# A norm moved out of the queries and into the exponential's scale, in a fused Mamba and local-attention kernel

## The reference, cut to what matters

```python
q = l2norm(q) * qs          # t / max(norm(t), 1e-12), per token and head
k = l2norm(k) * ksc
q, k = rotary_xpos(q, k)    # linear in q and in k
sim = einsum(q * 8.0, k)    # per head, 128 queries x 256 keys
sim = where(mask, -max, sim)
attn = softmax(sim)
out = einsum(attn, v)
```

## Time and profile before

| | us |
|---|---|
| median of 3 runs | 2109.19 (2108.12 to 2111.52) |
| the profiled execution, by the clock of the runs | 2109.78 |
| its span, first to last instruction | 2108.0 |
| PE busy | 1957.7 (93%) |
| DVE busy | 1866.4 (89%) |
| ACT busy | 1675.6 (79%) |
| POOL busy | 1094.0 (52%) |

### The profile page before, as it was taken

How to read it: one execution, slowest core, us unless ns; L and a number is a source line. 1 busy time by engine, 2 the same in 40 slices (tenths; PEclk the granted TensorE clock), 3 DMA queues, 4 the chain that set the end, 5 groups by cost and what they waited for, 6 DMA issues and landing times. The chain is left out here.

```text
span 2108.0 us, 40069 instructions
## 1 busy us (share of the span) xinstructions
PE 1957.7 (93%) x12096; PEld 1341.7 (64%) x12096; DVE 1866.4 (89%) x2502; ACT 1675.6 (79%) x4124; POOL 1094.0 (52%) x1214
## 2 busy tenths in 40 slices
PE   6788999999999999999999999999999999998897
PEld 2465666666666666666675666666666666665666
DVE  3988999999999999999989999999999999898881
ACT  4866888878878888888879788897887888887672
POOL 3544554655545655555555555465554565545440
PEclk9989999999999999999999999999999999999999
DMA  4788899789896898888987898978889789788772
GB/s 159 175 216 194 185 245 226 179 194 239 193 250 169 189 250 191 220 200 216 225 213 192 199 222 219 229 190 201 233 197 251 171 194 247 163 212 214 205 150 53
DMA packets 131844, 425.26 MB, mean 202 GB/s; under 512 B 13584, under 2 KB 34832, under 8 KB 113072
## 3 DMA queue, kind: packets, MB, share of 16 engines
q0 software_dynamic: 64512, 184.58, 47.8%
q1 hardware_dynamic: 67120, 238.12, 33.8%
HBM read 241.76 MB, written 155.71 MB: 189 GB/s over the span
## 5 line engine op out<-in xcount | busy, mean ns | idle before, releaser
L761 DVE TENSOR_TENSOR_SCAN hb<-dA,state,hb 128x512 f32<-128x512 f32 x512 | 668.5, 1306 | 36.3 <-ACT dA L934 20.8
L1170 POOL DMA_DIRECT2D ysum<-dA x256 | 222.6, 878 | 375.4 <-DVE dA L768 343.8
L934 ACT ACTIVATE dA<-dt_sb,par 128x512 f32<-128x512 f32 x512 | 349.2, 729 | 12.4 <-DMA ysum<-dA 11.1
L1154 POOL COPY state<-hb 128x2 f32<-128x2 f32 x256 | 207.4, 810 | 255.4 <-DVE hb L761 255.4
L754 DVE TENSOR_TENSOR hb<-u_sb,bc 128x1024 f32<-128x1024 f32 x256 | 316.0, 1234 | 25.6 <-DMA bc<-bc_rows 11.5
L768 DVE TENSOR_TENSOR dA<-hb,bc 128x1024 f32<-128x1024 f32 x256 | 312.2, 1220 | 0.0
L1485 PE MATMUL ring<-hT,w 128*128 128x256 f32 x1280 | 294.9, 388 | 5.2 <-ACT hT L1082 4.1
L1036 ACT ACTIVATE rot<-rot,rnorm 128x64 f32<-128x64 f32 x1024 | 256.5, 341 | 45.1 <-POOL rnorm L1239 43.3
L1485 PEld LDWEIGHTS ring<-hT,w 128*128 128x128 f32 x1280 | 243.9, 193 | 56.3 <-ACT hT L1082 19.0
L1239 POOL TENSOR_TENSOR rnorm<-rnorm,powers 128x8 f32<-128x8 f32 x128 | 265.5, 2075 | 23.5 <-POOL rnorm L1236 22.2
L1061 ACT ACTIVATE probs<-ring,nmax 128x256 f32<-128x256 f32 x512 | 234.8, 481 | 34.5 <-DVE nmax L840 34.1
(11 more groups left out here) (122 smaller groups left out, 3536.9 us busy)
## 6 DMA issues: line engine op xcount, KB each, us to landing
bc<-bc_rows SPq DMA_DIRECT2D x128, 1024.0 KB, 6.0
ysum<-dA POOLq DMA_DIRECT2D x256, 512.0 KB, 7.3
rot<-sq POOLq DMA_DIRECT2D x128, 256.0 KB, 6.3
wqkv<-in_wqkv SPq DMA_DIRECT2D x48, 512.0 KB, 7.3
w<-in_w SPq DMA_DIRECT2D x16, 1408.0 KB, 11.2
w<-in_w SPq DMA_DIRECT2D x16, 896.0 KB, 10.8
tab<-in_tab SPq DMA_DIRECT2D x64, 128.0 KB, 8.4
wo<-in_wo SPq DMA_DIRECT2D x16, 512.0 KB, 9.9
```

The source lines that it names most:

```text
L761: dve.tensor_tensor_scan(hb[:, k % H_RING, :], dA[:, k % DA_RING, :], hb[:, k % H_RING, :], state[:, k:k + 1], ALU.mult, ALU.add).then_inc ...
L934: act.activation(dA[:, k % DA_RING, :], dt_sb[:, j, :], ACT.Exp, scale=par[:, C_ALOG + n:C_ALOG + n + 1]).then_inc(dA_ready.sem, 1)
```

## The change: what it does, and the diff

The scores are linear in q, so 1/norm of a query can be applied to a whole row of scores. The change leaves the queries unscaled: ACT's `turn` runs for k only, and PE transposes q as soon as the two products of the rotation are added. The exponential takes 1/norm of its query and head as its scale, exp(scale * score - scale * maximum). For its bias the negated row maximum must be scaled too; that is a new small DVE product on 128x4 numbers, `mr` (function `scale_max`), two for a window, into a new buffer `shifts`. It waits for the two row maxima, for q's 1/norm, and for the exponentials of the window before, and ACT's `e` waits for it. q's 1/norm is now needed until the last exponential, so it has two buffers that alternate, and POOL's `turn(q,a)` waits for the exponentials of window a-2 where it waited for ACT's norm of window a-1. The tables of all five engines are new.

```diff
-    rnorm = sb("rnorm", [P, 2 * HEADS])
+    rnorm = sb("rnorm", [P, 3 * HEADS])
+    shifts = sb("shifts", [P, HEADS])
...
+            def scale_max(a, c):
+                dve.wait_ge(*nmax_ready.at(it, a * PAIRS + 2 * c + 2))
+                dve.wait_ge(*rnorm_ready.at(it, 2 * a + 1))
+                dve.wait_ge(*probs_ready.at(it, (a - 1) * HEADS + 4 * c + 4))
+                part = slice(4 * c, 4 * c + 4)
+                slot = a % 2 * HEADS + 4 * c
+                dve.tensor_tensor(shifts[:, part].rearrange("p (o h) -> p o h", o=2),
+                                  nmax[:, part].rearrange("p (o h) -> p o h", o=2),
+                                  rnorm[:, slot:slot + 4].rearrange("p (h o) -> p o h", o=2), ALU.mult).then_inc(shifts_ready.sem, 1)
...
-            def norm_heads(name, a):
+            def norm_heads(a):
-                i = "qk".index(name)
+                i = 1
...
                     act.activation(rot[:, i, h * DH:(h + 1) * DH], rot[:, i, h * DH:(h + 1) * DH], ACT.Copy,
-                                   scale=rnorm[:, i * HEADS + h:i * HEADS + h + 1]).then_inc(normed.sem, 1)
+                                   scale=rnorm[:, 2 * HEADS + h:2 * HEADS + h + 1]).then_inc(normed.sem, 1)
...
             def exps(a, g):
                 c, hh = divmod(g, 2)
-                act.wait_ge(*nmax_ready.at(it, a * PAIRS + 2 * c + 2))
+                act.wait_ge(*shifts_ready.at(it, 2 * a + c + 1))
...
-                                   bias=nmax[:, 2 * p + hh:2 * p + hh + 1], accum_out=rowsum[:, head:head + 1])\
+                                   bias=shifts[:, 2 * p + hh:2 * p + hh + 1],
+                                   scale=rnorm[:, a % 2 * HEADS + head:a % 2 * HEADS + head + 1], accum_out=rowsum[:, head:head + 1])\
...
             def scale_heads(name, a):
...
-                pool.wait_ge(*normed.at(it, HEADS * (n - 1)))
+                if i:
+                    pool.wait_ge(*normed.at(it, HEADS * a))
+                else:
+                    pool.wait_ge(*probs_ready.at(it, HEADS * (a - 1)))
...
             def heads(a):
                 for i, name in ((1, "kT"), (0, "qT")):
-                    pe.wait_ge(*normed.at(it, HEADS * (2 * a + i + 1)))
+                    if i:
+                        pe.wait_ge(*normed.at(it, HEADS * (a + 1)))
+                    else:
+                        pe.wait_ge(*rot_added[0].at(it, D16 * (a + 1)))
```

The tables move nearly every row. Of DVE's steady table, one line before and after:

```diff
-stats(3) +scan +scan +m(0,0) +m(0,1) +turn(q,1) +m(0,2) +m(0,3) +scan gate(1) +scan h(3,0) h(3,1) +scan
+o(7) +scan stats(3) +scan +scan +m(0,0) +m(0,1) +mr(0,0) +turn(q,1) +turn(k,1) +m(0,2) +m(0,3) +mr(0,1)
```

More of the change, by code:

```diff
@@ L94 @@
[L94 to L98, removed]
@@ L102 @@
++scan +h(2,0) +h(2,1) +rinv(6) +h(2,2) +h(2,3) +gate(0) +h(2,4) +h(2,5) +scan +scan
 """
 ACT_ORDER = """
-+dA heads(7) +dA +q(0) v(7) e(7,0) e(7,1) +k(0) pT(7,0) e(7,2) e(7,3) pT(7,1) pT(7,2) pT(7,3) rb(7) +dA +dA
-wo(6) +dA wo(7) +turn(q,0) +turn(k,0) +heads(0) hn(3) +v(0) +q(1) hT(3) +e(0,0) +e(0,1) +dA +dA +dA +e(0,2)
-+e(0,3) +dA h(3,0) h(3,1) last(3) +dt(2) +dt(3) +k(1) h(3,2) h(3,3) h(3,4) h(3,5) +dA +dA +dA +dA +dA
-+pT(0,0) w2(3) +pT(0,1) +turn(q,1) +turn(k,1) +pT(0,2) +pT(0,3) +dA +rb(0) +dA +dA +start(0) +dA +heads(1)
@@ new lines @@
++e(0,3) h(3,0) h(3,1) h(3,2) h(3,3) h(3,4) h(3,5) last(3) +dt(2) +dt(3) +dA +turn(k,1) +dA +dA +dA +pT(0,0)
++pT(0,1) +q(2) +k(2) +dA w2(3) +dA +dA +heads(1) +rb(0) +start(0) +pT(0,2) +pT(0,3) +dA +dA +z(0) +z(1)
++z(2) +dA +e(1,0) +turn(k,2) +e(1,1) +dA +v(1) +e(1,2) +e(1,3) +pT(1,0) +pT(1,1) +wo(0) +dA +dA +z(3)
++start(1) +pT(1,2) +rb(1) +skip(1) +pT(1,3) +heads(2) +dA +q(3) +v(2) +e(2,0) +e(2,1) +wo(1) +e(2,2) +e(2,3)
++k(3) +pT(2,0) +pT(2,1) +hn(0) +pT(2,2) +dA +pT(2,3) +hT(0) +dA +dA +dA +rb(2) +dA +h(0,0) ++xn(0) +last(0)
@@ new lines @@
++add(4) +add(5) +turn(q,2) +scan +add(6) +rot(q,2) +rot(k,2) +scan +turn(k,2) +scan +add(7) +add(8) +scan
++scan +add(9) ++norm(0) +scan +q(3) +add(10) +rot(q,3) +stats(0) +rot(k,3) +add(11) +scan +turn(q,3)
++turn(k,3) +scan +add(12) +scan +add(13) ++norm(1) ++halo +carry +add(14) +q(4) +scan +scan +scan +add(15)
++add(16) +add(17) +turn(q,4) +rot(q,4) +rot(k,4) +turn(k,4) +skip(1) +scan +stats(1) +scan +add(18) +add(19)
++q(5) +scan +rot(q,5) +rot(k,5) ++tail +scan +q(6) +add(20) +turn(q,5) +add(21) +turn(k,5) +scan +scan
@@ L182 @@
+e(6,3) v(6) hT(2) q(7) k(7) h(2,0) pT(6,0) pT(6,1) dA dA dA dA h(2,1) h(2,2) pT(6,2) pT(6,3) h(2,3) h(2,4)
+h(2,5) rb(6) last(2) +dA +dA turn(k,7) w2(2)
 """
 POOL_FIRST = """
-q(0) norm(0) norm(1) rot(q,0) rot(k,0) halo turn(q,0) turn(k,0) q(1) turn(q,1) turn(k,1) rot(q,1) rot(k,1)
-scan q(2) scan add(0) add(1) rot(q,2) skip(0) scan rot(k,2) turn(q,2) scan add(2) add(3) q(3) scan turn(k,2)
-+norm(0) scan add(4) add(5) +norm(1) add(6) scan turn(q,3) rot(q,3) rot(k,3) turn(k,3) add(7) scan stats(0)
@@ new lines @@
+turn(k,1) scan scan add(0) q(2) add(1) rot(q,2) turn(q,2) rot(k,2) scan skip(0) +norm(0) q(3) turn(k,2) scan
+add(2) add(3) scan add(4) rot(q,3) scan +halo scan add(5) add(6) scan rot(k,3) add(7) turn(q,3) scan
+turn(k,3) stats(0) scan add(8) add(9) +norm(1) scan scan add(10) add(11) scan add(12) add(13) carry scan
+scan q(4) add(14) add(15) scan scan scan add(16) add(17) rot(q,4) rot(k,4) turn(q,4) scan q(5) skip(1)
+turn(k,4) stats(1) scan scan add(18) add(19) rot(q,5) rot(k,5) add(20) add(21) turn(q,5) turn(k,5) scan scan
```

317 lines of the change are left out of this document (158 added, 159 removed).

## The result

The changed kernel takes 2155.28 us, median of 4 runs (2152.77 to 2158.74). The kernel before, run beside it, takes 2108.65 us (2106.87 to 2111.52). The ratio is 1.0217, with a 95% interval of 1.0196 to 1.0237: slower by 46 us, where 15 us less was forecast, and beyond the upper end of the range. The profiled execution took 2153.5 us, its span 2151.7.

A forecast was written before the change was run, and what follows sets the result against it. PE was taken as the bound, DVE second, with ACT holding PE up most. 2109.8 - 27.6 (norm waits) + 12 (products) = 2094.2, forecast as 2094 us, 0.7% faster; the forecast's own range 2080 to 2104, the whole range 2068 to 2122.

The forecast's parts named there:

- the other queues: POOL, transfers, SP and PE: work stays the same, SP's table only moves its starts; nothing booked.
- The gross gain of 27.6 us: PE's waits for ACT's norm of q and k all go: 27.6 us over the span, ends 0 and 73.
- a sign of being wrong: On PE, the wait for the norm stays since POOL's power still comes last.
- The exponentials: On ACT, 512 run 0.09 us longer each, 46 us in all; nothing booked since PE has other work queued.
- The products: On DVE, 128 new products cost about 24 us; half, 12 us, charged to the span, ends 0 and 29.
- The clock: On PE, granted clock 0.99 over a pass, so TensorE is nearly throughout at 2.4 GHz and the clock no lever.
- The bound: PE is full first (239.6 of 250 us), DVE second (231.8), in a loop where ACT holds PE up most.
- The second rival: DVE becomes the bound between row maxima and next scan: slower, 2130, or 2118 with half the waits avoidable; chance 0.24.
- The first rival: PE's norm wait moves to the layer norm's output and elsewhere; all 15.6 us comes back, 2110 (2106 to 2113); chance 0.16.

The follow-up runs named there:

- w2_late: Changed kernel with SP's load of w2 issued behind the 7th bc load instead of in front of w1's load and the 5th bc load; 2114.42 us, ratio 1.0036.
- before_meet: Kernel before with only SP's steady table changed: loads of w2 and w1 issued together right in front of the 5th bc load; 2094.49 us, ratio 0.994.
- nd_kfirst: Kernel before without ACT's norm of q, and on POOL k's power in front of q's where k's transfer is already out; 2088.04 us, ratio 0.9905.
- tables_only: Kernel before's arithmetic (ACT scales q and k, no products) on the changed kernel's tables; 2142.22 us, ratio 1.0162.
- products_only: Kernel before with 128 additional DVE products on 128x4, two a window behind the row maxima, results unused; 2122.95 us, ratio 1.0066.

## Why the prediction was wrong, point by point

**The step that failed most** is the one on the other queues: "The transfers are the same in number. SP's table only moves its starts", booked at 0. It is 38 of the 46 us: after less w2_late. The prediction counted the transfers and did not ask how much room each has. What the runs showed in its place is one bc load a pass that lands after 16.4 us with 9.9 us of room, a wait of 6.5 us on DVE and 6.3 us lost on PE. Part of it was readable ahead of time. In the kernel before the fifth bc load has 11.9 us from issue to use and takes 4.8. The new SP table puts 2.3 MB of weights between the fourth and the fifth load, where the old one has 1.4. What it cost could not be read exactly, since before_meet shows the pair in front of a bc load without a wait; that it could cost a wait could. The Trainium skill, page "DMA: Bandwidth & Descriptors", section "Issuing engines are not separate DMA queues", says that transfers from all issuers run on the same 16 engines and interleave. The trace agrees: while SP's load of 1 MB took its 16.4 us, POOL's transfers had 60.3% of the 16 engines' time. The same page's section "Bandwidth" has 6.15 us for 1 MB issued from GpSimd; the 4.8 us measured in the kernel before, for a load issued from SP, is below that.

**The gross gain of 27.6 us** was booked as if nothing came back in its place. PE's wait for the norm did fall on the new tables, by 10 us over the span and by 3.5 us a pass, but other waits grew by more. In w2_late, between 200 and 1900 us, the wait for the norm is 6.3 us (26.4 before), the waits for the exponentials are 19.6 + 4.0 us (2.7 before) and that for the Mamba layer norm 10.3 us (none of note before). PE is idle for 80.0 us of 1700 there, in before for 73.4, by these two rows (before, w2_late). On the old tables the relief of ACT alone is -2 us (-5 to +1), where POOL's power of k came last and stood behind q's. The prediction had said so for windows 1 and 2 and had named it as a sign of being wrong; nd_kfirst bears it out, with -20 us once k goes first.

```profile
200.00:1900.00 1700.00, 1626.56 (x10194) 1119.22 (x10192) 1577.06 (x2116) 1417.99 (x3494) 922.65 (x1009) 0.99 0.86 209
```

```profile
200.00:1900.00 1700.00, 1619.99 (x10201) 1117.39 (x10199) 1591.31 (x2220) 1346.23 (x3054) 934.64 (x1014) 1.00 0.84 210
```

**The exponentials** were right in size and wrong in place. 0.09 us each was worked out, 569 - 481 = 88 ns was measured. They were booked at nothing "since PE has other work queued there". Alone they cost 28 us, 60% of the 47 us by which ACT's exponentials grow. The 0.2 us of the earlier trace rows said that PE hardly waited for exponentials; it did not say how near it was to waiting. On the new tables most of the wait for them came with the tables alone (16.9 us in tables_only, 19.6 in w2_late). The Trainium skill, page "ScalarE: Activation LUTs", section "What ACT_TABLE_LOAD costs", gives about 93 ns for each pointer operand, and the trace agrees within 5 ns; the page says nothing of where they land.

**The products** were the best term: 12 us charged, 14 measured (9 to 19). DVE's busy time grew by 22 us in the kernel after and by 20 in products_only, and a product lasts 0.16 us in the median.

**The clock** was called no lever, from a granted clock of 0.99 over a pass. The runs contradict it: the wait of 2.60 us in window 2, priced at 2.60, carries 1.67 us of slower matmuls behind it in the pass read above, and before_meet gains 12.6 us with nearly all of it in PE's busy time. In the kernel after PE is busy 14.9 us longer than in w2_late for the same matmuls. This did not decide the sign, but it is a cost of long waits that the sum left out.

**The bound** was read as PE first and DVE second, with the waits between them as a loop. What the runs add is how much of a change on another engine reaches the end: 14 of 20 us on DVE, 28 of 47 on ACT, and 2 of 128 on ACT where POOL came last. The parts taken alone sum to 14 + 28 - 2 = 40 us, and the arithmetic together is 30 (24 to 35).

**The rivals.** The second rival (slower, DVE becomes the bound, 2118 to 2130) had the sign right, but its mechanism is not what happened: DVE's share in the period fell from 92.7% to 235.26 / 258 = 91.2%. Without the late load, in w2_late, it is 1591.31 / 1700 = 93.6%, and the loss is 8 us. The first rival (the wait moves, 2106 to 2113) describes what remains in w2_late, at 2114, better than it describes the changed kernel. What no rival held was a transfer that comes late.

## What to carry to other kernels

Before a table of DMA starts is moved, list for each load that the pacing engines need the room from its issue to its use (with two buffers that is what the using engine does in between) and what is still on its way when it is issued, from every queue; a share of busy DMA engines near 1.0 doesn't tell a load that is late from one that isn't. To shorten an engine is worth nothing while what it waits for next stands in the same place: read the releaser of that engine's own waits first, and move that. A longer instruction on an engine with free time isn't free if the pacing engine's next step consumes its result. And a long wait of PE costs more than its length where the granted clock falls behind it: compare PE's busy time for the same matmuls before a difference of 1% is put down to anything else.

## What the runs showed of the hardware that was not expected

The same 1 MB load, in traces of five orders of the transfers, took 4.8, 7.7, 11.1, 11.2 and 16.4 us from issue to landing. The share of the DMA engines was 0.96 in the slowest case and 1.05 in the second fastest. A wait of PE of 4.7 us was followed by a granted clock of 0.51 and 0.63, and the 24 matmuls behind it cost 1.6 us more than at the upper level. Behind one wait of 2.60 us it was 0.58, and four matmuls cost 1.67 us more. A power on 128x8 numbers took POOL 2.58 us at one place of the pass and, with two loads of SP moved, 1.67.
